# One program for attention and FFN, block 0's first layer in the drain, and DVE's turn ahead of its move

## The chip, the core and the metric

The kernel runs on one core of one Trainium2 chip. Its engines are PE (matmul), ACT (activation functions, copies), DVE (elementwise and reductions), POOL (a second elementwise engine) and SP (which only issues DMAs here). Each follows its own instruction stream in order, and semaphores tie the streams together. The metric is the device time of one execution in microseconds.

## What is computed

32 x 256 = 8192 tokens of width 128 go through attention over a memory of 4096 slots, a layer norm, a feed-forward network of width 512 and a second layer norm.

```python
q = x @ Wq.T + bq
scores = einsum('bshd,hmd->bshm', q, memory_keys) / sqrt(128)      # 8192 x 4096
probs = softmax(scores, axis=-1)
x = layernorm(x + (probs @ memory_values) @ Wo.T + bo)
h = silu((x @ w1.T) * s1) * ((x @ w2.T) * s2)                      # 128 -> 512
h = gelu((h @ h1.T) * s_h1)                                        # 512 -> 512
h = gelu((h @ h2.T) * s_h2)                                        # 512 -> 512
x = layernorm(x + (h @ w3.T) * s3)                                 # 512 -> 128
```

## The kernel before

**Two programs.** `program` calls `attention` and then `ffn`. Each opens its own block of engine programs, so all engines finish the first before any starts the second.

**Attention** works on 32 pairs of row tiles (2 x 128 tokens). `frames` runs one frame for each pair and three more to drain: frame f computes the scores of pair f while the parts of pairs f-1 and f-2 pass through the later stages. A frame has 16 steps t and, for DVE and SP, 8 slots j = 4 x tile + k, one for each piece of 1024 score columns. Frames 0 to 3 and from 28 on are written out; those between are a loop of two frames.

- *PE* (`frame`, L693): in each step three matmuls of scores (L711 to L713, high and low halves of queries and keys), and after two steps the value products of two steps of pair f-2 (`add_values`, L685 to L690). At t = 8 it projects the next pair's queries (L664).
- *DVE* (`frame`, L597): in slot j it moves the scores of piece j from PSUM to `rows` with their maximum (L608; I call it the move, M), once the previous pair's content of these rows has been sent. After the fourth move of a tile it finds the row maximum and the bias (L614, L616). Then comes the turn (T, a transpose in 32 x 32 squares, L577) of a piece that Exp has finished, by `turned_piece(f, j)`: slot 0 turns (tile 0, k 3) of the previous pair, slots 1 to 4 its tile 1, slots 5 to 7 pieces (0,0) to (0,2) of this pair.
- *SP* (`exchange`, L404): it waits for each turned piece and sends it in four DMAs of 128 KB within the SBUF from `rows` to `slot_p`, which has two halves, one for each parity of the pair. Before the first piece of a pair it waits until POOL has used up the half (L412). It also loads the queries' input and stores the outputs of pair f-3.
- *ACT* (`frame`, L508): in each step it converts a part of `slot_p` to 16 bits (`high_part`, L506; part 0 waits for all eight pieces), at even steps an Exp of a piece (L497), at t = 8 the next queries (L476).
- *POOL* (L454): the low half of each part, what the conversion lost. PE's value products need both.

The order within a step on ACT is high part, then Exp, so Exp (0,0) at t = 8 stands ahead of high part 11 of the pair before.

**Drain.** In frames 32 to 34 the last Exps, turns and exchanges of pair 31 are done, ACT issues the last exchange itself (L550), POOL makes the low halves of pair 30, DVE all of pair 31 (`last_low_part`, L582). DVE, POOL and PE already prepare the first layer norm of blocks 0 and 1.

**FFN** works on 16 blocks of 512 tokens. `turn(i)` runs, for PE, the first layer (w1, w2) of block i+1, the output transposes of block i+2, the layer h2 of block i, h1 of block i+1 and w3 of block i. Turn -1 fills the pipeline: first layer and h1 of block 0. A value read from memory (`low_max`) tells whether the weights need a low half; with these inputs they don't. DVE and PE each branch on it at the head of `ffn`.

## Time and profile before

| | |
|---|---|
| median of 3 runs | 1143.17 us (1141.53 to 1144.19) |
| the profiled execution | 1143.68 us |
| its span, first to last instruction | 1141.9 us |
| PE busy | 1092.9 us, 96% |
| DVE busy | 963.5 us, 84% |
| ACT busy | 905.3 us, 79% |
| POOL busy | 645.3 us, 57% |
| mean granted clock of PE | 0.995 |

The runs take 1.8 us more than the span from the first to the last instruction. Busy shares are means over two parts with different loads: attention to about 772 us, the FFN from 774 us on. Matmul ends are modelled by the profile, so a PE that is counted busy is not at its peak; the starts are measured.

### The profile page before, as it was taken

What the parts mean: (1) busy time and instruction counts of PE and PEld (TensorE: products, weight loads), DVE (VectorE), ACT (ScalarE), POOL (GpSimd) and SP (SyncE); (2) the same over time, 40 slices, a digit from 0 to 9 for tenths busy, and PEclk for the clock granted to TensorE, in tenths of its full rate; (3) what the DMA queues carried; (4) which work ended last, traced back from release to release, by engine and by line L of the source; (5) the groups of instructions that cost most, each with busy time, mean ns of one, the idle gap of its engine ahead of it and who ended that gap; (6) DMA issues with size and microseconds to landing.
All of it is one profiled execution on the core that took longest, in us unless ns stands there. A gap on an engine that the chain in (4) does not pass through costs nothing. (4 is left out here: it accounts for less than half of the span.)

```text
span 1141.9 us, 20141 instructions
## 1 busy us (share of the span) xinstructions
PE 1092.9 (96%) x5324; PEld 769.4 (67%) x5324; DVE 963.5 (84%) x1803; ACT 905.3 (79%) x1610; POOL 645.3 (57%) x618
## 2 busy tenths in 40 slices
PE   7799999999999999999999999988999999999996
PEld 5566666666666666666666666635787887888775
DVE  6888898998899889998998899875787887888874
ACT  6788788878887887788878877777788878888883
POOL 1487788878877887888778878760211121121110
PEclk9999999999999999999999999999999999999999
DMA  6878888888888888888888988854020111001000
GB/s 199 190 186 200 200 201 205 206 197 204 201 195 195 202 200 199 200 206 202 200 194 208 207 186 198 186 124 166 1 56 28 28 48 34 28 28 55 11 10 29
DMA packets 83942, 165.90 MB, mean 145 GB/s; under 512 B 19648, under 2 KB 47808, under 8 KB 83776
## 3 DMA queue, kind: packets, MB, share of 16 engines
q1 hardware_dynamic: 79824, 161.50, 59.8%
q10 hardware_dynamic: 4080, 3.94, 1.2%
q8 instruction: 18, 0.29, 0.1%
q14 instruction: 20, 0.16, 0.0%
HBM read 22.76 MB, written 8.39 MB: 27 GB/s over the span
## 5 line engine op out<-in xcount | busy, mean ns | idle before, releaser
L454 POOL TENSOR_TENSOR pT<-slot_p,pT 128x512 f16<-128x512 f32 x496 | 561.9, 1168 | 143.5 <-ACT pT L506 143.5
L608 DVE TENSOR_SCALAR_CACHE_REDUCE rows<-s_ps 128x1024 f32<-128x1024 f32 x256 | 310.8, 1214 | 72.9 <-DMA slot_p<-rows 48.3
L506 ACT ACTIVATE pT<-slot_p 128x512 f16<-128x512 f32 x512 | 296.1, 617 | 84.1 <-DMA slot_p<-rows 76.2
L577 DVE STREAM_TRANSPOSE rows<-rows 128x1024 f32<-128x1024 f32 x256 | 317.0, 1239 | 2.1 <-ACT rows L497 2.1
L497 ACT ACTIVATE rows<-rows,bias 128x1024 f32<-128x1024 f32 x256 | 291.6, 1139 | 15.7 <-DVE bias L616 15.4
L711 PE MATMUL s_ps<-keys,q_buf 128*128 128x512 f32 x512 | 249.6, 488 | 7.7 <-DVE rows L608 4.8
L685 PE MATMUL o_ps<-pT,v_hi 128*128 128x512 f16 x512 | 198.1, 387 | 21.2 <-POOL pT L454 20.9
L990 PE MATMUL ring<-h_hi,w_all 128*128 128x512 f32 x512 | 205.6, 402 | 1.7 <-DVE h_lo L936 1.4
L712 PE MATMUL s_ps<-keys,q_buf 128*128 128x512 f32 x512 | 203.4, 397 | 0.0
L991 PE MATMUL ring<-h_lo,w_all 128*128 128x512 f32 x512 | 202.3, 395 | 0.0
L713 PE MATMUL s_ps<-keys,q_buf 128*128 128x512 f32 x512 | 202.1, 395 | 0.0
L688 PE MATMUL o_ps<-pT,v_lo 128*128 128x256 f16 x1024 | 196.1, 273 | 0.0
L690 PE MATMUL o_ps<-pT,v_hi 128*128 128x512 f16 x512 | 194.6, 380 | 0.0
L162 POOL TENSOR_TENSOR var_eps<-moments,eps 128x4 f32<-128x4 f32 x32 | 6.8, 213 | 305.0 <-DVE moments L183 305.0
L688 PEld LDWEIGHTS o_ps<-pT,v_lo 128*128 128x128 f16 x1024 | 101.0, 99 | 83.4 <-issue 0.8
L881 ACT ACTIVATE gelu<-ring,scales 128x512 f32<-128x512 f32 x128 | 88.0, 687 | 61.8 <-PE ring L991 61.8
L685 PEld LDWEIGHTS o_ps<-pT,v_hi 128*128 128x128 f16 x512 | 49.4, 97 | 117.1 <-POOL pT L454 66.1
L711 PEld LDWEIGHTS s_ps<-keys,q_buf 128*128 128x128 f32 x512 | 96.7, 189 | 27.4 <-issue 5.1
L990 PEld LDWEIGHTS ring<-h_hi,w_all 128*128 128x128 f32 x512 | 96.2, 188 | 25.4 <-DVE h_lo L936 2.6
L713 PEld LDWEIGHTS s_ps<-keys,q_buf 128*128 128x128 f32 x512 | 96.1, 188 | 23.3
L991 PEld LDWEIGHTS ring<-h_lo,w_all 128*128 128x128 f32 x512 | 96.3, 188 | 21.6
L712 PEld LDWEIGHTS s_ps<-keys,q_buf 128*128 128x128 f32 x512 | 96.7, 189 | 17.5
(95 smaller groups left out, 1202.1 us busy)
## 6 DMA issues: line engine op xcount, KB each, us to landing
slot_p<-rows SPq DMA_DIRECT2D x1020, 128.0 KB, 2.4
x_in<-in_xT SPq DMA_DIRECT2D x32, 128.0 KB, 2.5
x_in<-in_x SPq DMA_DIRECT2D x16, 256.0 KB, 3.6
o_scratch<-o_sum SPq DMA_DIRECT2D x32, 128.0 KB, 2.0
out<-y_out SPq DMA_DIRECT2D x16, 256.0 KB, 2.4
o_in<-o_scratch SPq DMA_DIRECT2D x14, 256.0 KB, 3.3
z<-in_w_all ACTq DMA_DIRECT2D x25, 113.0 KB, 3.1
rows<-in_w_all SPq DMA_DIRECT2D x1, 2816.0 KB, 12.5
```

Of the source, the lines that this page charges most:

```text
L454: nc.gpsimd.tensor_tensor(halves(s % RING, 1), slots_first(pp, s), halves(s % RING, 0), ALU.subtract).then_inc(split, 1)
L497: nc.scalar.activation(s, s, ACT.Exp, bias=bias[:, tile:tile + 1], scale=SCALE, accum_out=den[:, bass.ds((2 * p + tile) * PIECES + k, 1)]) ...
L506: nc.scalar.activation(halves(s % RING, 0), slots_first(pp, s), ACT.Copy).then_inc(highed, 1)
L577: nc.vector.transpose(row_piece(tile, k), row_piece(tile, k)).then_inc(turned, 1)
L608: nc.vector.tensor_scalar(row_piece(tile, k), s_ps[:, j % 2, :], 1.0, None, ALU.mult, ALU.max, accum_out=part_max[:, tile, k:k + 1]).then_ ...
L685: nc.tensor.matmul(o_ps[:, pp, :], v_hi[:, 2 * s, :], pT[:, s % RING, 0, :], start=s == 0, stop=False, skip_group_check=True)
L688: nc.tensor.matmul(o_ps[:, pp, 0:2 * P], v_lo[:, 2 * s + c, :], pT[:, s % RING, c, 0:2 * P], start=False, stop=False, skip_group_check=True)
L711: nc.tensor.matmul(out, q_h, k_h, start=True, stop=False)
L712: nc.tensor.matmul(out, q_h, k_l, start=False, stop=False)
L713: last = nc.tensor.matmul(out, q_l, k_h, start=False, stop=True)
L990: nc.tensor.matmul(out, wh, hh, start=n == 0, stop=False)
L991: last = nc.tensor.matmul(out, wh, hl, start=False, stop=final and not low_weights)
```

## The change

There are three parts.

1. `attention` and `ffn` become one function `layers` with one block, so no engine waits for all others between them. The branch on `low_max` moves: PE's now stands behind frame 31, DVE has none, POOL has one. The load of the raw weights waits for the last exchanges.
2. The first layer of block 0 moves into the drain. PE does its first half behind value step 11 of pair 30 (`FIRST_LAYER_STEP`), the other half behind step 15, and h1 behind the values of pair 31. Frames 32 to 34 are written out by engine: DVE makes the low parts of pair 30 from step 12 on (`LATE_STEP`), ACT issues the last two exchanges, and ACT's gates and DVE's products of block 0 stand between high and low parts. They use free columns of `rows`. In later blocks `prod` is written over `gate`.
3. In each slot of a frame DVE turns its piece ahead of its move of scores.

Shown without the changed indentation, and cut; turns of the FFN are the same but for names and for block 0, which they no longer start:

```diff
+LATE_STEP = 12
+FIRST_LAYER_STEP = 11
...
-            for f in range(PAIRS - 4, PAIRS + 3):
+        for f in range(PAIRS - 4, PAIRS):
                 frame(f, f % 2)
...
+    def product(b, j):
+        return rows[:, (2 + j % 2) * BT:(3 + j % 2) * BT] if is_step(b, 0) else gate[:, j, :]
...
 # SP, behind its frames
+        exchange(PAIRS - 1, 1, 0, PIECES - 1)
+        exchange(PAIRS - 1, 1, 1, 0)
+        exchange(PAIRS - 1, 1, 1, 1)
+        stage.store_output(sp, PAIRS - 3)
...
+        for tile in range(2):
+            for k in range(PIECES):
+                sp.wait_ge(sent[tile][k], 16 * GROUPS * PAIRS)
+        sp.dma_start(raw, w_raw[:, 0:W_COLS]).then_inc(raw_loaded, 16)
...
 # POOL, behind its frames
+        for s in range(STEPS - T_LAG, LATE_STEP):
+            low_part(PAIRS - 2, 0, s)
             stage.inverse_deviation(pool, 1, 0)
+        pool.wait_ge(stage.low_found, 1)
+        low = pool.value_load(stage.low_max[0:1, 0:1].bitcast(I32))
+        with pool.If(low > 0):
...
+        with pool.Else():
+            nc.gpsimd.memset(table_room[:, 1:2], 0.0).then_inc(w_split, 2)
...
 # ACT, behind its frames
+        for s in range(STEPS - T_LAG, 6):
+            high_part(PAIRS - 2, 0, s)
+            if s == 3:
+                stage.output_half(act, PAIRS - 3, 1)
+        for k in range(PIECES):
+            exp_piece(PAIRS - 1, 1, k)
+        for s in range(6, STEPS):
+            high_part(PAIRS - 2, 0, s)
+            if s == 7:
+                act.wait_ge(sent[0][0], 16 * GROUPS * PAIRS)
+                stage.keep_x1T(act, 0)
+            for k in (2, 3):
+                if s == (11, 14)[k - 2]:
+                    act.wait_ge(turned, 8 * (PAIRS - 1) + PIECES + k + 1)
+                    send(act, 1, 1, k)
+        load_table(ACT.Silu)
+        act.wait_ge(stage.scales_loaded, 16 * len(scale_cols))
+        for k in (1, 2):
+            act.wait_ge(sent[0][k], 16 * GROUPS * PAIRS)
+        for j in range(2):
+            gate_of(0, j)
+        for j in range(2):
+            product_high(0, j)
+        stage.output_half(act, PAIRS - 2, 0)
+        for s in range(STEPS):
+            high_part(PAIRS - 1, 1, s)
+            if s == 8:
+                gate_of(0, 2)
+            if s == 11:
+                gate_of(0, 3)
+            if s == 13:
+                load_table(ACT.Gelu)
+                product_high(0, 2)
+        product_high(0, 3)
+        stage.output_half(act, PAIRS - 1, 1)
+        stage.keep_x1T(act, 1)
+        gelus(0, 1, mid1_done, (mid2_done, 0))
+        turns(act, turn)
...
 # DVE, in each slot of a frame
+                if valid(before[0], PAIRS):
+                    turn_piece(*before)
                     if valid(f, PAIRS):
 
                         dve.wait_ge(scored, 8 * f + j + 1)
...
-                    if valid(before[0], PAIRS):
-                        turn_piece(*before)
...
 # DVE, behind its frames
+        turn_piece(PAIRS - 1, 0, PIECES - 1)
+        turn_piece(PAIRS - 1, 1, 0)
+        stage.output_sum(dve, PAIRS - 3, 1)
+        for k in range(1, PIECES):
+            turn_piece(PAIRS - 1, 1, k)
                         stage.split_x1(dve, 0)
+        for s in range(LATE_STEP, STEPS):
+            low_part(PAIRS - 2, 0, s)
+        stage.residual(dve, 1)
+        dve.wait_ge(stage.scales_loaded, 16 * len(scale_cols))
+        for j in range(2):
+            product_of(0, j)
+        for j in range(2):
+            product_low(0, j)
                         for s in range(STEPS):
-                            last_low_part(s, 1 - par)
+            low_part(PAIRS - 1, 1, s)
+            if s == 5:
                         stage.normalise_x1(dve, 1)
+            if s == 8:
+                product_of(0, 2)
+            if s == 11:
+                product_of(0, 3)
+            if s == 13:
+                product_low(0, 2)
+        product_low(0, 3)
+        stage.output_sum(dve, PAIRS - 2, 0)
+        stage.output_sum(dve, PAIRS - 1, 1)
+        stage.sum_rows(dve, READY_TILES, TILES, 1)
+        dve.wait_ge(stage.rden_ready, 2)
+        gelu_low(0, 1, 0)
+        gelu_low(0, 1, 1)
+        stage.split_x1(dve, 1)
+        gelu_low(0, 1, 2)
+        gelu_low(0, 1, 3)
+        turns(dve, turn)
...
 # PE, behind its frames
+        def last_values(low_weights):
+
+            for s in range(STEPS):
+                add_values(PAIRS - 2, 0, s)
+                if s == (STEPS - 1 if low_weights else FIRST_LAYER_STEP):
+                    pe.wait_ge(scores_moved, 8 * PAIRS)
+                    pe.wait_ge(stage.w_rounded, CHECKS)
+                    pe.wait_ge(stage.x1_split, 1)
+                    if low_weights:
+                        pe.wait_ge(w_split, 1)
+                    first_layer(0, (0, 1), low_weights)
+            first_layer(0, (2, 3), low_weights)
+            for s in range(STEPS):
+                add_values(PAIRS - 1, 1, s)
+            stage.turn_x1(pe, 1)
+            if low_weights:
+                pe.wait_ge(w_split, 2)
+            for j in range(HC):
+                bank_read_by_in(0, j)
+                layer(ring[:, j, :], "h1", j, 0, mid1_done, low_weights, parts_ready=(in_split, 0))
+
+        pe.wait_ge(stage.low_found, 1)
+        low = pe.value_load(stage.low_max[0:1, 0:1].bitcast(I32))
+        with pe.If(low < 1):
+            last_values(False)
+            turns(pe, lambda i, i2, par: turn(i, i2, par, False))
```

## Rows read from the trace of the kernel before

**Rows 1.** The windows of a stretch of attention and of one FFN turn.

```profile
500.00:650.00 150.00, 148.28 (x756) 98.36 (x753) 135.84 (x207) 123.87 (x233) 122.66 (x112) 1.00 0.87 202
...
833.50:855.50 22.00, 22.00 (x102) 17.64 (x101) 17.99 (x50) 18.07 (x29) 3.71 (x5) 1.00 0.13 36
```

**Rows 2.** The waits of 100 to 600: total us, times, longest.

```profile
DVE rows L608 <- DMA slot_p<-rows: 36.6, 41, 1.9
...
PE o_ps L685 <- POOL pT L454: 8.7, 18, 0.8
ACT rows L497 <- DVE bias L616: 8.3, 14, 0.9
```

**Rows 3.** SP's own waits, 100 to 600, then 640 to 760.

```profile
SPq L376 <- POOL pT L454: 13.0, 20, 1.0
SPq L376 <- DVE rows L577: 7.7, 24, 0.6
...
SPq L376 <- DVE rows L577: 7.1, 8, 2.0
```

**Rows 4.** The timeline of one frame, 400 to 427, four engines.

```profile
403.83 1.22 DVE L608 TENSOR_SCALAR_CACHE_REDUCE rows<-s_ps 128x1024 f32<-128x1024 f32 x1 [1.79 <-DMA slot_p<-rows]
...
407.95 1.15 ACT L497 ACTIVATE rows<-rows,bias 128x1024 f32<-128x1024 f32 x1 [0.86 <-DVE bias L616]
...
409.79 5.65 POOL L454 TENSOR_TENSOR pT<-slot_p,pT 128x512 f16<-128x512 f32 x5 [2.21 <-ACT pT L506]
...
415.46 3.05 SPq L376 DMA_DIRECT2D slot_p<-rows  x5
...
426.97 1.22 DVE L608 TENSOR_SCALAR_CACHE_REDUCE rows<-s_ps 128x1024 f32<-128x1024 f32 x1 [1.86 <-DMA slot_p<-rows]
```

**Rows 5.** DVE's timeline: first and last of 21 such moves.

```profile
174.78 1.23 DVE L608 TENSOR_SCALAR_CACHE_REDUCE rows<-s_ps 128x1024 f32<-128x1024 f32 x1 [0.87 <-DMA slot_p<-rows]
...
630.90 1.23 DVE L608 TENSOR_SCALAR_CACHE_REDUCE rows<-s_ps 128x1024 f32<-128x1024 f32 x1 [0.83 <-DMA slot_p<-rows]
```

**Rows 6.** PE's timeline: the first matmul of two neighbouring slots.

```profile
406.14 0.58 PE L711 MATMUL s_ps<-keys,q_buf 128*128 128x512 f32 x1
...
408.85 0.59 PE L711 MATMUL s_ps<-keys,q_buf 128*128 128x512 f32 x1
```

**Rows 7.** The timeline around a frame's end, ACT and DVE.

```profile
416.52 0.63 ACT L506 ACTIVATE pT<-slot_p 128x512 f16<-128x512 f32 x1 [2.18 <-DMA slot_p<-rows]
417.06 1.14 ACT L497 ACTIVATE rows<-rows,bias 128x1024 f32<-128x1024 f32 x1
...
419.65 1.23 DVE L608 TENSOR_SCALAR_CACHE_REDUCE rows<-s_ps 128x1024 f32<-128x1024 f32 x1 [0.43 <-DMA slot_p<-rows]
```

**Rows 8.** The timeline of the drain, engine by engine.

```profile
748.88 11.81 POOL L454 TENSOR_TENSOR pT<-slot_p,pT 128x512 f16<-128x512 f32 x10 [1.88 <-ACT pT L506]
...
749.86 1.08 DVE L198 SCALAR_TENSOR_TENSOR z<-y_ps,rden,xb 128x128 f32<-128x128 f32 x4
...
759.96 10.30 DVE L582 TENSOR_TENSOR pT<-slot_p,pT 128x512 f16<-128x512 f32 x16 [5.83 <-ACT pT L506]
770.18 1.10 DVE L188 TENSOR_SCALAR x<-z,moments,rstd 128x128 f32<-128x128 f32 x4
...
775.75 0.75 DVE L930 SCALAR_TENSOR_TENSOR prod<-ring,scales,gate 128x512 f32<-128x512 f32 x1 [0.89 <-ACT gate L865]
...
753.47 2.19 ACT L506 ACTIVATE pT<-slot_p 128x512 f16<-128x512 f32 x4 [1.59 <-PE o_ps L690]
...
768.11 1.28 ACT L553 ACT_TABLE_LOAD   x1
...
774.05 0.49 PE L990 MATMUL ring<-keys,w_all 128*128 128x512 f32 x1 [2.09 <-DVE spare L914]
...
775.45 0.63 PE L991 MATMUL ring<-keys,w_all 128*128 128x512 f32 x1
...
789.41 0.40 PE L990 MATMUL ring<-keys,w_all 128*128 128x512 f32 x1
```

More of the change, by code:

```diff
@@ new lines, in layers @@
+    wo_power, wo_scale, wo_scaled = (stage.xb[:, n, :] for n in range(3))
+    ident, v_unscale, o_ps = stage.ident, stage.v_unscale, stage.o_ps
+    spare_half = slot_p[:, 1, :, :, :].rearrange("p a c t -> p (a c t)")
+    k_raw = spare_half[:, 0:SLOTS]
+    v_in = spare_half[:, SLOTS:2 * SLOTS]
+    v_raw = k_raw
+    s_ps = ctx.enter_context(nc.psum_tensor("s_ps", [P, 2, PIECE], FP32))
+    q_ps = stage.x1_ps
+    k_loaded = [sem(f"k_loaded{n}") for n in range(K_PARTS)]
+    v_loaded = [sem(f"v_loaded{n}") for n in range(PIECES)]
@@ new lines, in part_step, with value_halves, checking, check_part @@
+    def part_step(f, t, lag):
+        return (f - 1, t - lag) if t >= lag else (f - 2, t + STEPS - lag)
+    def value_halves(f, t):
+        step = t - V_STEP + STEPS * f if isinstance(f, int) else -1
+        return (step,) if 0 <= step < HALVES else ()
+    def checking(f):
+        return not isinstance(f, int) or 0 <= f - FIRST_CHECK < CHECKS
+    def check_part(f):
+        return stage.w_all[:, bass.ds((f - FIRST_CHECK) * CHECK_COLS, CHECK_COLS)]
+    def slots_first(pp, s):
+        return slot_p[:, pp, :, 2 * s:2 * s + 2, :].rearrange("p a c t -> p c a t")
@@ new lines, in halves, with k_part, frames, send @@
+    def halves(t, low):
+        return pT[:, t, :, low * 2 * P:(low + 1) * 2 * P].rearrange("p c (a t) -> p c a t", t=G)
+    def k_part(t, n):
+        return half_piece(t, n) if n < 2 else piece(t, n - 1)
+    def frames(eng, frame):
+        for f in range(4):
+            frame(f, f % 2)
+        with eng.Fori(2, PAIRS // 2 - 2) as half:
+            frame(half * 2, 0)
+            frame(half * 2 + 1, 1)
+        for f in range(PAIRS - 4, PAIRS):
+            frame(f, f % 2)
+    def send(eng, pp, tile, k):
+        for g in range(GROUPS):
+            eng.dma_start(slot_p[k * G:(k + 1) * G, pp, tile * GROUPS + g, :, :].rearrange("p c t -> p (c t)"),
+                          row_piece(tile, k)[g * G:(g + 1) * G, :]).then_inc(sent[tile][k], 16)
@@ new lines, in layers @@
+    ctx.close()
+    ctx = hold
+    w_hi = stage.w_all[:, 0:W_COLS]
+    in_room = keys[:, 2 * BT:2 * BT + 2 * HC * BT].rearrange("p (a k n) -> p a k n", a=2, k=HC)
+    w_lo_in = keys[:, 2 * BT + 2 * HC * BT:2 * BT + 2 * HC * BT + W_AT["h1"]]
+    w_lo_rest = sb("w_lo_rest", [P, W_COLS - W_AT["h1"]], FP32R)
+    raw = rows[:, 2 * SLOTS - W_COLS:]
+    x1T, x1_hi, x1_lo, scales, table_room = stage.x1T, stage.x1_hi, stage.x1_lo, stage.scales, stage.table_room
+    gelu = sb("gelu", [P, 2, HC, BT], FP32)
@@ L1050, in turn @@
-                if valid(i, BLOCKS):
-                    at_least(pe, z2T_ready, i)
-                    layer(y3_ps[:, :], "w3", 0, 2, y3_done, low_weights, P, (gelu_split[1], 4 * i))
-            with pe.If(stage.low_of["PE"] < 1):
-                turns(pe, lambda i, i2, par: turn(i, i2, par, False))
-            with pe.Else():
-                turns(pe, lambda i, i2, par: turn(i, i2, par, True))
+                        bank_read_by_in(i + 1, j)
+                    else:
+                        pe.wait_ge(gelu_h[0], 4 * i + j + 1)
@@ L1072, in program @@
         stage = RowStage(nc, stage_ctx, t["x"].rearrange(tiled, p=P), o_dram, o_stored, den, keys, rows)
[L1073 to L1075 removed]
+        layers(nc, stage, stage_ctx, t["xT"], t["wqT"], t["bq"], t["kT"], t["vT"], t["woT"], t["bo"], scale_cols, t["w_all"],
+               den, keys, rows, out.rearrange(tiled, p=P))
 def kernel(**inputs):
```

1246 lines of the change are left out of this document (580 added, 666 removed).

## The prediction

> **What bounds the kernel now.** I read the windows first. In the attention part every engine but PE has idle time, and PE is counted busy nearly throughout; in the FFN part PE is busy in 22.00 of 22.00 us and nothing else is near that [rows 1]. So an FFN turn costs 22.0 us as long as PE is fed, and the diff changes nothing inside a turn: sixteen turns stay as they are. What can move is the period of a pair of row tiles in attention, and the drain between the last scores and the first FFN turn.
>
> The period comes from the starts of one instruction in successive frames: DVE's move of the third piece of scores, which I call M2. Its starts run from 174.78 to 630.90 with 20 periods between, so 22.81 us a pair [rows 5]. PE could do it in less: one slot (scores of a piece, then two value steps) starts 2.71 us after the one before [rows 6], eight make 21.7 us, the projection of the next queries adds about 0.4 (my estimate from one slot that holds it), so PE's floor is about 22.1 to 22.2 us. The period is 0.6 to 0.7 above it.
>
> Next the waits, for what holds the period up. Over 500 us (22 pairs) PE waits 8.7 us for the low half of the probabilities, 0.40 a pair; DVE waits 36.6 us for the landing of exchanges, 1.7 a pair; ACT waits for the bias before an Exp in 14 pairs [rows 2]. SP, which issues 32 exchanges of 128 KB a pair, idles only 0.35 us a pair for a turn of DVE and 0.6 for POOL [rows 3]. Nearly everything is close to full, so single idle times prove little and a closed loop has to be found.
>
> The timeline gives one [rows 4]. M2 starts at 403.83, when the previous pair's piece (0,2) has left its rows. A turn, the next move M3, the maximum and the bias follow, and ACT's Exp of piece (0,0) starts at 407.95. Behind this Exp in ACT's order stands high part 11, behind that POOL's last five subtracts: they start at 409.79 and take 5.65, to 415.44. They free the half of slot_p, and SP, which waited for exactly that, issues (0,0) at 415.46. Then come (0,1), an input and (0,2), and its landing starts M2 of the next frame at 426.97. That is 4.12 + 1.84 + 5.65 + 11.53 = 23.14 us, all of this pair's period and no other engine in it. Where the bias is waited for (14 of 22 pairs) this loop is the bound; in the rest PE's query projection arrives a little later than the bias and decides.
>
> **The change, part by part.**
>
> *DVE's turn ahead of its move.* The cyclic order of M and T (turn) is the same, each T steps over one M, so each T can be done one move earlier, up to 1.2 us. Gain on the last exchange (1,3): SP loses its 0.35 us a pair of waiting for DVE, high part 0 starts that much sooner, and the 0.40 us a pair that PE waits at the second value step mostly goes. But in the loop above nothing gets shorter: M2 waits for the DMA in every frame, and between M2 and M3 there still stands one T, now (1,2) in place of (1,1). What PE gains it will wait for M2 or M3 in the scores. I cost the edit at zero in the pairs that the loop binds and at about 0.15 us (estimate) in the 8 of 22 that PE's projection binds, so -1 us over the main part. Its lower bound is the PE floor (rival B), its upper bound a T that waits for its Exp and holds up the M behind it (rival D).
>
> In the unrolled frames 28 to 31 DVE carries extra work (block 0's residual and statistics), and SP waits for turns 7.1 us between 640 and 760, up to 2.0 at a time, part of it in the drain [rows 3]. Turns that are one move early give back between 0 and 4 of this; the loop above still stands behind it, so I take 1.5, nearer to the low end.
>
> *The drain, before.* POOL's ten subtracts for steps 6 to 15 of pair 30 run from 748.88 for 11.81 us; DVE then does all 16 of pair 31 from 759.96 for 10.30; then a normalisation, 1.10. PE has its last value step done at 774.05 - 2.09 = 771.96, waits 2.09 through the end of the first program and the branch of the second, and only then begins block 0's first layer; turn 0 proper, block 1's first layer, begins at 789.41 [rows 8]. At 775.45 a matmul takes 0.63: the granted clock of that stretch is at the lower of the two levels (1.2 GHz) after the pause, and that costs about 1.5 us before 779. So 17.4 us pass between the last value step and turn 0.
>
> *The drain, after.* POOL ends its share with step 11, at 748.88 + 6 x 1.18 = 756.0. PE puts the first half of block 0's first layer behind step 11 (8 matmuls, 1.9 us by the rate of a turn), then steps 12 to 15 (0.65 each, as two fill about half of a slot of 2.71 [rows 6]), to about 761.2. ACT now issues two pieces between its high parts; today's one cost it 1.59 us ahead of high part 12, seen at 753.47 [rows 8]. The second should cost 1.6 to 3 more, since its sequencer runs ahead I take high part 15 done at 757.1. Then the table load 1.28 (row at 768.11) and two gates, done at 759.3 and 760. DVE does lows 12 to 15 to 757.7, then the residual, whose combinations take 1.08 [rows 8] and the statistics about as much again (estimate 2.4 in all, 760.1), two products of 0.75, to 761.7. ACT's copies and its output half follow, two subtracts of up to 0.75 run beside them, and high part 0 of pair 31 is ready at about 763.4. This is 3.5 us later than today's 759.96.
>
> From there DVE sets the pace: 10.30 + 1.10 + three operations of 0.75 (products 2 and 3, one low part) = 13.65 us, to 777.1; PE's last value step follows at 777.7. So the values end 5.8 us later than before. What is behind them is shorter: no pause of 2.09, no first layer of block 0, only block 1's transposes (0.5) and 32 matmuls of the second layer. A turn has 102 instructions, 88 of them of this size, in 22.00 us [rows 1], so one is 0.22 to 0.25 and 32 take 6.9 to 8.0; I take 7.6. The 16 of the first layer that are gone from here were 3.5 to 4.0, and 1.5 more by the clock. Turn 0 begins at 785.9 instead of 789.41: -3.5 us. With each estimate above at its better or worse end this is -6.5 to 0.
>
> The cover of what I cost at nothing: PE's value load and branch now stand ahead of pair 30's values. All of today's pause, 2.09, bounds them, and PE would be at most 0.7 late for step 0; the steps come at POOL's 1.18 each and PE needs 0.65, so it has caught up by the third. The Trainium skill (Runtime: NRT & Kernel Launch, Instruction fetch mechanics) says that a taken branch whose target is not in the fetched window stalls the engine for a fetch. That speaks for a price at the new place too; by it the sum stays the same, because of the cover. The trace shows only the pause of 2.09, barrier and branch together. POOL's branch and its memset have nothing waiting in this path; the raw weights' load, now behind the landing of all exchanges, is needed only in turn 1.
>
> *Sum.* -1.0 - 1.5 - 3.5 = -6.0. The span of 1141.9 becomes 1135.9, the profiled execution's 1143.68 becomes 1137.7. The median of the runs is 0.5 below that execution, so **1137**.
>
> **The rivals.** Differences under 0.2% (2.3 us) can hardly be told from no change.
>
> A, as above: 1132 to 1140.9. For it: M2 waits for the DMA in all the frames I followed. Chance 0.54.
>
> B, the attention period falls. If the loop has slack that I misread (landing after (0,2) shorter when (1,3) has left the queues sooner), the period can fall from 22.81 towards PE's 22.2: 0.6 x 27 = 16 us at most, to 1121; half of it gives 1129. For it: PE's wait and SP's for DVE are both removed, and every engine has idle time. Against it: the stretch from SP's (0,0) to M2 holds the same three pieces. Chance 0.18.
>
> C, the drain gives nothing. DVE's 13.65 us are a chain with ACT's gates; if gates wait for the late issue of two pieces, or the granted clock falls to the lower level in the DVE-paced values as at 775.45, the 3.5 us go, and with them part of the rest: 1140 to 1144. Chance 0.17.
>
> D, slower. One mechanism: T(0,3) now stands ahead of M0. Its Exp starts only after high part 0, which waits for the exchange: 416.52, Exp 417.06 to 418.19, T to 419.4, and M0 starts at 419.65 [rows 7]. The margin is 0.2 us. If the Exp slips by x, M0 and M1 slip by x - 0.2, but M2 has 1.7 us of waiting in hand, so this decides only from x of about 1.5 on. At 2 us a pair it costs 0.3 x 27 = 8 us: 1145 to 1149. Chance 0.11.
>
> Faster: A 0.54, B 0.18, a part of C 0.03, together 0.75. Same: the rest of C, mostly, 0.13. Slower: D and a little of C, 0.12. The range takes in A, nearly all of C and the nearer half of B: 1125 to 1143; A alone is 1132 to 1141.
>
> **What would show it.** M2's starts stay 22.6 to 22.8 us apart, with the DMA as what it waited for, while PE's wait for POOL at the second value step shrinks below 0.15 a pair and SP's wait for DVE nearly vanishes. DVE's 16 last subtracts start at 763 to 764 less the shift of about 2.5 that comes from ahead, and PE's first matmul of block 1 comes about 6 us earlier than 789.41. A period of 22.3 would prove the loop wrong; a DVE wait for L497's Exp ahead of a turn in most frames would be rival D; a lower granted clock between 760 and 785 or a PE pause over 1 us behind the last value step would be C.

## The result, and the profile after

The changed kernel takes 1125.84 us, median of 4 runs (1123.78 to 1126.36); the kernel before took 1142.9 beside it (1141.53 to 1144.19). The ratio is 0.9848, 95% interval 0.983 to 0.9865: 17.1 us less, where 6.0 were predicted. The range of 1125 to 1143 holds the time by 0.8 us, but the likeliest case, A (1132 to 1140.9), does not. The profiled execution has a span of 1122.1 us against 1141.9, so 19.8 us less.

The windows of the changed kernel, in the columns of [rows 1]: the same stretch of attention, and one turn of the FFN.

```profile
core 0: us, PE busy (x) PEld busy (x) DVE busy (x) ACT busy (x) POOL busy (x), PEclk, DMA share, GB/s
500.00:650.00 150.00, 147.95 (x761) 99.65 (x761) 135.63 (x205) 124.64 (x233) 125.72 (x115) 1.00 0.89 205
819.81:841.56 21.75, 21.75 (x101) 17.64 (x100) 17.96 (x50) 18.07 (x30) 3.71 (x5) 1.00 0.13 36
```

PE is busy throughout in both, as before. The turn, however, is 21.75 long and not 22.00. Its waits from 100 to 600, to be read against [rows 2]:

```profile
DVE rows L812 <- DMA slot_p<-rows: 27.3, 45, 1.5
...
PE o_ps L972 <- POOL pT L542: 7.5, 12, 0.8
...
ACT rows L613 <- DVE bias L820: 3.6, 11, 1.0
```

SP's own waits in that stretch, against [rows 3]:

```profile
SPq L377 <- POOL pT L542: 13.9, 16, 1.3
SPq L377 <- DVE rows L779: 9.8, 30, 0.6
```

I had said that SP's wait for DVE would nearly vanish and PE's for POOL shrink from 0.40 a pair to 0.15. Neither happened: 9.8 in place of 7.7 us, and 7.5 in place of 8.7. What became less is DVE's wait for the DMA (36.6 to 27.3) and ACT's for the bias (8.3 to 3.6).

The starts of M2, the move that the prediction took the period from, against [rows 5] (the same 20 periods):

```profile
172.53 1.22 DVE L812 TENSOR_SCALAR_CACHE_REDUCE rows<-s_ps 128x1024 f32<-128x1024 f32 x1 [1.52 <-DMA slot_p<-rows]
...
622.79 1.22 DVE L812 TENSOR_SCALAR_CACHE_REDUCE rows<-s_ps 128x1024 f32<-128x1024 f32 x1 [1.05 <-DMA slot_p<-rows]
```

That is 22.51 us a pair, in place of 22.81. I had expected 22.6 to 22.8, and 22.3 as the proof that the loop is wrong; it lies between the two.

For a ledger I cut each trace at three marks: ACT's conversion of the queries of pair 4 and of pair 31 (`q_buf`), and the transposes into `y_ps` in turn 0. The marks of before, ACT's timeline:

```profile
63.55 0.47 ACT L476 ACTIVATE q_buf<-x_ps,bq_col 128x256 fp32r<-128x256 f32 x1 [1.52 <-PE x_ps L664]
85.85 0.47 ACT L476 ACTIVATE q_buf<-x_ps,bq_col 128x256 fp32r<-128x256 f32 x1 [1.18 <-PE x_ps L664]
...
705.84 0.47 ACT L476 ACTIVATE q_buf<-x_ps,bq_col 128x256 fp32r<-128x256 f32 x1 [1.22 <-PE x_ps L664]
```

And of the changed kernel, with three neighbouring pairs of the loop:

```profile
61.79 0.47 ACT L592 ACTIVATE q_buf<-x_ps,bq_col 128x256 fp32r<-128x256 f32 x1 [0.95 <-PE x_ps L951]
83.87 0.48 ACT L592 ACTIVATE q_buf<-x_ps,bq_col 128x256 fp32r<-128x256 f32 x1 [1.76 <-PE x_ps L951]
...
581.40 0.47 ACT L592 ACTIVATE q_buf<-x_ps,bq_col 128x256 fp32r<-128x256 f32 x1 [1.29 <-PE x_ps L951]
603.57 0.47 ACT L592 ACTIVATE q_buf<-x_ps,bq_col 128x256 fp32r<-128x256 f32 x1 [1.70 <-PE x_ps L951]
626.30 0.47 ACT L592 ACTIVATE q_buf<-x_ps,bq_col 128x256 fp32r<-128x256 f32 x1 [1.29 <-PE x_ps L951]
...
695.84 0.48 ACT L592 ACTIVATE q_buf<-x_ps,bq_col 128x256 fp32r<-128x256 f32 x1 [1.22 <-PE x_ps L951]
```

The `y_ps` transposes of turn 0 start at 791.50 before and at 776.31 after. So the 19.8 us are: 2.0 ahead of pair 4, 8.0 in the 27 periods to pair 31 (620.0 to 612.0), 5.2 from there to turn 0 (85.7 to 80.5), and 4.6 in the FFN (350.4 to 345.8). From about pair 10 to the end of the loop every other period is now 22.17 us, which is the PE floor of 22.1 to 22.2 that the prediction worked out, and the ones between are 22.7 to 23.0.

### The profile page after: what moved, and what is told of

Its sections match the earlier page's. It is cut to its first block, busy times and chain, and to the rows that moved or that the text cites. A ratio compares the mean times of both kernels' runs of the same rounds, so it can differ in the third digit from the quotient of the medians.

```text
span 1122.1 us, 20046 instructions
## 1 busy us (share of the span) xinstructions
PE 1081.3 (96%) x5324; PEld 770.6 (69%) x5324; DVE 968.3 (86%) x1806; ACT 905.3 (81%) x1609; POOL 642.1 (57%) x615
## 4 chain that ended last, share of the span: by engine, by line
PE 36%; SPq 15%; ACT 13%; issue 10%; DVE 9%; POOL 8%; DMA 7%; ACTq 1%; DVEq 0%; POOLq 0%
SPq L377 14%; PE ring L1045 12%; PE ring L1046 12%; POOL pT L542 7%; ACT rows L613 7%; DMA slot_p<-rows 6%; ACT pT L622 5%; DVE rows L812 3%; DVE rows L779 3%; PE o_ps L1045 1%; PE o_ps L1046 1%; PE s_ps L1000 1%; PE s_ps L998 1%; PE s_ps L999 1%; PE o_ps L972 1%
## 5 line engine op out<-in xcount | busy, mean ns | idle before, releaser
L542 POOL TENSOR_TENSOR pT<-slot_p,pT 128x512 f16<-128x512 f32 x482 | 545.7, 1166 | 130.5 <-ACT pT L622 130.5
L812 DVE TENSOR_SCALAR_CACHE_REDUCE rows<-s_ps 128x1024 f32<-128x1024 f32 x256 | 308.6, 1205 | 51.8 <-DMA slot_p<-rows 34.7
L613 ACT ACTIVATE rows<-rows,bias 128x1024 f32<-128x1024 f32 x256 | 291.7, 1140 | 12.6 <-DVE bias L820 12.0
L975 PEld LDWEIGHTS o_ps<-pT,v_lo 128*128 128x128 f16 x1024 | 101.1, 99 | 84.2 <-issue 0.6
L1045 PE MATMUL ring<-keys,w_all 128*128 128x512 f32 x384 | 153.3, 399 | 1.0 <-ACT gate L669 0.9
L1046 PE MATMUL ring<-keys,w_all 128*128 128x512 f32 x384 | 150.5, 392 | 0.0
L1000 PEld LDWEIGHTS s_ps<-keys,q_buf 128*128 128x128 f32 x512 | 96.3, 188 | 22.7
L876 DVE TENSOR_TENSOR h_lo<-gelu,h_hi 128x512 fp32r<-128x512 f32 x128 | 81.9, 688 | 26.5 <-ACT h_hi L698 26.3
L1045 PE MATMUL ring<-h_hi,w_all 128*128 128x512 f32 x256 | 103.1, 403 | 0.3 <-ACT gate L669 0.3
```

The costliest lines, as they stand in the source:

```text
L542: nc.gpsimd.tensor_tensor(halves(s % RING, 1), slots_first(pp, s), halves(s % RING, 0), ALU.subtract).then_inc(split, 1)
L613: nc.scalar.activation(s, s, ACT.Exp, bias=bias[:, tile:tile + 1], scale=SCALE, accum_out=den[:, bass.ds((2 * p + tile) * PIECES + k, 1)]) ...
L812: nc.vector.tensor_scalar(row_piece(tile, k), s_ps[:, j % 2, :], 1.0, None, ALU.mult, ALU.max, accum_out=part_max[:, tile, k:k + 1]).then_ ...
L975: nc.tensor.matmul(o_ps[:, pp, 0:2 * P], v_lo[:, 2 * s + c, :], pT[:, s % RING, c, 0:2 * P], start=False, stop=False, skip_group_check=True)
L1000: last = nc.tensor.matmul(out, q_l, k_h, start=False, stop=True)
L1045: nc.tensor.matmul(out, wh, hh, start=n == 0, stop=False)
```

## The experiments

The runs came in groups, each on one chip, and the kernel before reads 1138.2 to 1143.1 us in median from group to group. So times are compared by their ratio to the before of the same group, and stretches by the traces. This is the ledger of all profiled runs, in us (cut as above; "order" is DVE's, new is turn ahead of move):

| run | order, programs | to pair 4 | pair 4 to 31 | to turn 0 | FFN | ratio (95%) |
|---|---|---|---|---|---|---|
| before | old, 2 | 85.85 | 620.0 | 85.7 | 350.4 | 1 |
| g1_before_again | old, 2 | 86.19 | 616.6 | 87.4 | 350.7 | 0.9998 (0.998 to 1.0015) |
| e6_pad_alone | old, 2 | 86.02 | 618.8 | 87.3 | 350.2 | 0.9983 (0.9966 to 1.0001) |
| f1_ffn_edits_alone | old, 2 | 87.45 | 613.9 | 85.6 | 345.7 | 0.9957 (0.994 to 0.9973) |
| e1_reorder_alone | new, 2 | 84.47 | 614.4 | 84.2 | 350.4 | 0.9954 (0.9939 to 0.9969) |
| e2_order_undone | old, 1 | 85.74 | 613.1 | 82.2 | 345.7 | 0.9895 (0.9878 to 0.9911) |
| f2_order_undone_no_pad | old, 1 | 87.85 | 615.5 | 81.0 | 346.3 | 0.9922 (0.9905 to 0.994) |
| f3_order_at_start_only | both, 1 | 84.13 | 614.0 | 81.5 | 345.8 | 0.9901 (0.9885 to 0.9918) |
| changed kernel | new, 1 | 83.87 | 612.0 | 80.5 | 345.8 | 0.9848 (0.983 to 0.9865) |
| e5_changed_again | new, 1 | 84.05 | 612.4 | 80.8 | 345.8 | 0.9859 (0.9831 to 0.9887) |
| h2_changed_control | new, 1 | 84.73 | 613.1 | 81.0 | 346.0 | 0.9851 (0.9837 to 0.9865) |
| e3_two_waits_more | new, 1 | 83.99 | 612.5 | 80.2 | 347.3 | 0.9878 (0.9861 to 0.9894) |
| e4_own_room | new, 1 | 84.45 | 611.9 | 81.1 | 347.9 | 0.9886 (0.9869 to 0.9902) |
| e7_no_pad | new, 1 | 84.04 | 614.0 | 80.0 | 345.9 | 0.9862 (0.9834 to 0.989) |
| e8_small_work_later | new, 1 | 84.33 | 613.3 | 79.9 | 345.7 | 0.9859 (0.9831 to 0.9887) |
| f4_h2_high_in_keys | new, 1 | 84.45 | 613.5 | 80.4 | 344.8 | 0.9867 (0.9851 to 0.9884) |
| g2_pool_all_lows | new, 1 | 84.16 | 613.0 | 79.8 | 345.9 | 0.9869 (0.9851 to 0.9888) |
| g3_sp_sends_one_more | new, 1 | 84.10 | 611.4 | 80.3 | 345.7 | 0.9855 (0.9834 to 0.9875) |
| g4_first_layer_behind | new, 1 | 85.38 | 613.9 | 87.0 | 345.6 | 0.9917 (0.9895 to 0.9939) |
| h1_both | new, 1 | 84.28 | 613.1 | 79.9 | 345.7 | 0.9845 (0.9831 to 0.986) |

**The order of DVE, alone and taken back.** e1 is the kernel before with the turn ahead of the move; e2 is the changed kernel with this undone:

```diff
                 if j == PIECES and valid(f + 1, PAIRS):
                     q_low_part(f + 1, 1 - par)
+                if valid(before[0], PAIRS):
+                    turn_piece(*before)
                 if valid(f, PAIRS):
                     ...
-                if valid(before[0], PAIRS):
-                    turn_piece(*before)
```

> The kernel before with DVE's reorder alone (turn ahead of move in each slot), two programs, drain and FFN as before. Theory P (the one-frame loop of the prediction: M2, bias, Exp (0,0), high part 11, POOL, SP (0,0), landing, M2): 1 to 2.5 us less than before, about 1141. Theory Q (a chain over two frames: M3, bias, query low part, then T(1,3), its exchange, high part 0, sixteen low parts of POOL, SP (0,0), M2; before, M4 stood in it ahead of T(1,3)): the whole attention gain of the change, 2 at the start and 0.27 a pair, so about 10 us less, 1133, and frames of 22.2 and 22.9 us in turn. If the gain needs one program, nothing here.

> The changed kernel with DVE's move of scores ahead of the turn again, all else of the change kept. Theory Q: the 10 us of attention come back, about 1136, period 22.8. Theory P: 1 to 2.5 come back, about 1128. What is left against before is the worth of the drain and the FFN: 5.2 + 4.6 by the two traces, so 9.8 less than before (1133) if these add up independently of the order, and 3.5 if the drain is worth what was predicted and the FFN nothing.

e1 took 1134.78 against 1139.83, 5.05 less, and e2 1128.33, 11.5 less. Their sum, 16.6, is about what the whole change saves (17.1 in its own group, 16.5 in that of e5), so the order on one side and drain with FFN on the other add up. Neither theory had the size of e1: P said 1 to 2.5, Q about 10. The stretch ahead of pair 4 is settled by these and by the next run.

**Where the order acts.** f3 keeps the new order in frames 0 to 3 and has the old one behind.

```diff
-                if valid(before[0], PAIRS):
+                if valid(before[0], PAIRS) and isinstance(f, int) and f < 4:
                     turn_piece(*before)
...
+                if valid(before[0], PAIRS) and not (isinstance(f, int) and f < 4):
+                    turn_piece(*before)
```

> The changed kernel with the new order of DVE in frames 0 to 3 only, the old one in the loop and behind. Theory O: of the 3.0 us between the changed kernel and the old order, 1.7 arise in frames 2 to 4 (frame 3's queries at 61.8 instead of 63.5), 0.7 in the loop and the rest in the drain: about 1126.6 if the start's gain is kept. Rival P (the loop absorbs what the start gains, since all stages wait for each other): 1128.3, as with the old order everywhere.

It took 1127.18. All six kernels with the old order at the start have pair 3's queries 24.2 to 25.7 us after pair 2's, and all with the new one, f3 too, 22.4 to 22.5: a gain of 1.7 or more that is still there at pair 4 (f3 reaches it at 84.13). Whether it lasts to the end the times don't tell: f3's ratio, 0.9901, lies between those of e2 and f2, which have the old order everywhere. The rows of POOL's first low part show how. Before:

```profile
51.23 1.16 POOL L454 TENSOR_TENSOR pT<-slot_p,pT 128x512 f16<-128x512 f32 x1 [13.18 <-ACT pT L506]
```

After:

```profile
48.87 1.16 POOL L542 TENSOR_TENSOR pT<-slot_p,pT 128x512 f16<-128x512 f32 x1 [10.73 <-ACT pT L622]
```

POOL's first low part is 2.4 us earlier; it starts at 51.2 to 51.8 in all traces with the old order and at 48.9 to 50.3 in all with the new. My explanation, which no run takes apart, is that while the pipeline fills no loop of freed buffers stands behind the turns, so that an earlier turn brings the exchange, the high part and what follows forward.

**Is it a chain through T(1,3)?** e8 moves two small operations of DVE (0.39 and 0.47) from the stretch between bias and T(1,3) to slot 6.

```diff
-                if j == PIECES and valid(f + 1, PAIRS):
-                    q_low_part(f + 1, 1 - par)
...
-                if j == 3 and checking(f - 1):
+                if j == 6 and checking(f - 1):
...
+                if j == 6 and valid(f + 1, PAIRS):
+                    q_low_part(f + 1, 1 - par)
```

> The changed kernel with DVE's two small operations between bias and T(1,3) (maximum of the weight check, 0.39; query low part, 0.47) moved to slot 6 behind the move. Theory Q (two-frame chain through T(1,3)): the longer of the two frames, 22.9, comes down towards 22.17, by up to 0.37 a pair, so 4 to 10 us less than the changed kernel. Rival R (SP, which issues for about 21.4 of 22.5 us, or PE's floor is the bound): nothing, within 1 us.

> The changed kernel again, on the chip of the next three runs, as their reference. 0.9848 of before, so 1123 to 1126; turns of the FFN 21.73 apart, frames 22.17 and 22.9 in turn.

e8 took 1125.16, e5 1125.23. Theory Q, which I had formed after the result, fell: its chain got 0.86 us shorter and nothing moved.

**Addresses and chance.** `table_room` moves all buffers behind it by 32 bytes. e6 adds such a buffer to the kernel before, e7 and f2 take it out of the changed kernel and of e2.

```diff
         self.spare = sb("spare", [P, 2], FP32)
+        self.pad = sb("pad", [P, 2], FP32)
```

> The kernel before with nothing but an unused buffer of two float32 columns, declared where the change declares table_room. All later buffers of SBUF, those of attention among them (values, slot_p, pT, the queries), lie 32 bytes further, on multiples of 64 bytes, which they do not before. Theory A (the 32 bytes shorten attention: the changed kernel with the old order of DVE had 22.54 us a pair against 22.81 before, with the same instructions in the loop): about 7 us less than before, first layer etc. unchanged, matmul slots of 2.69 in place of 2.71. Rival: that gain comes from the one program or is chance, and this kernel runs as before.

> The changed kernel with table_room inside the buffer spare, so that nothing of attention is moved by 32 bytes. Theory A: the PE-bound frames take 22.28 in place of 22.17, as in the run with the reorder alone, and 3 us are lost against the changed kernel, which leaves about 1128. Rival: as the changed kernel.

> The changed kernel with DVE's old order and with table_room inside spare, so that attention has the old addresses and, instruction for instruction, the old streams as far as frame 31. Theory O (in one program the new order is worth 3 us, addresses 0.5 at most): 1128 to 1129, all runs within 1 us, attention 613 us from the queries of frame 4 to those of the last. Rival N (attention of the old order varies by chance from kernel to kernel, 613 to 620): anything to 1135, with a spread as wide as that of before (8 us).

> The kernel before, unchanged. Theory V (the attention of the old order varies from execution to execution, and the trace of before was near its slow end): between the queries of frame 4 and the last 613 to 617 us, not 620, and a time under 1141. Rival: 619 to 621 again, so that the gain against the kernels with the old order in one program is due to something that the one program changes.

e6: 1140.22 against 1141.7, no difference. e7: 1125.65, as e5. Only the PE-bound periods feel it, 22.28 (e1, e7) and 22.17 (with the 32 bytes), 0.11 in every other pair, about 1.5 us. f2 took 1130.39 with runs from 1127.93 to 1132.38, so the one program with the old order isn't always as steady as in e2 (1127.61 to 1128.55). g1, the kernel before unchanged, took 1141.89 and has 616.6 from pair 4 to 31. With the old order that stretch is thus 613 to 620 long whatever else changes, and [rows 5] come from its longest sample; with the new order it is 611.4 to 614.4. The two ranges overlap, so a single pair of traces says little about the order here.

**The FFN's turn.** e3 gives DVE back the two waits ahead of each product, e4 puts the parts of h1's input into buffers of their own, f1 makes the edits of the FFN alone in the kernel before.

```diff
 # e3
             dve.wait_ge(in_done, 8 * b + 2 * j + 2)
+            if not is_step(b, 0):
+                dve.wait_ge(prod_high, 4 * b + j - 3)
+                dve.wait_ge(in_split, 4 * b + j - 3)
 # e4
+    own_hi, own_lo = sb("h_hi0", [P, HC, BT], FP32R), sb("h_lo0", [P, HC, BT], FP32R)
 # f1
-        prod = sb("prod", [P, HC, BT], FP32)
-        h_hi = sb("h_hi", [P, 3, HC, BT], FP32R)
+        prod = gate
+        in_room = keys[:, SLOTS:2 * SLOTS].rearrange("p (a k n) -> p a k n", a=2, k=HC)
+        h_hi = [in_room[:, 0, :, :]] + [sb(f"h_hi{n}", [P, HC, BT], FP32R) for n in (1, 2)]
...
-                        at_least(dve, prod_high, 4 * b + j - 3)
-                        at_least(dve, in_split, 4 * b + j - 3)
```

f1 takes the keys' second half for that room, where the low parts of the weights would lie that these inputs don't need.

> The changed kernel with the two waits given back to DVE ahead of each product of blocks 1 to 15 (both always satisfied). Theory W (each wait instruction costs DVE about 0.07 us, and PE waits for the second product of a turn): 0.15 us a turn in 15 turns, 2.3 us more, about 1128, turn 21.9. Rival S (the shorter turn comes from where the operands lie): no change, 1126.

> The changed kernel with the high and low parts of the first layer's product in buffers of their own from block 1 on, in place of the room of the keys. Theory S (matmuls of layer h1 start 0.2275 apart when their operand lies in the keys' room and 0.2335 elsewhere): 0.12 to 0.19 us a turn, 2 to 3 us more, about 1128. Rival W: no change, 1126.

> The kernel before with two edits of the FFN alone: the product is written over the gate, so that DVE has two waits less ahead of each, and the parts of layer h1's input lie in the keys' room. Theory F (both together are the whole shortening of a turn, 0.14 + 0.15 us as the two runs that took one of them back showed): turns of 21.73 us, 16 x 0.3 = 4.6 us less than before, drain and attention as before, about 1137. Rival: a turn is shorter only in the one program, no change.

f1 took 1133.67 against 1138.22, 4.55 less, as expected. The ratios of e3 and e4 (0.9878 and 0.9886) are hardly apart from the changed kernel's, so for them the traces decide. The turns of the traces show both parts. Between the transposes into `y_ps` and those of `z2T` stands the second half of the first layer. DVE's rows there, before:

```profile
837.29 1.41 DVE L930 SCALAR_TENSOR_TENSOR prod<-ring,scales,gate 128x512 f32<-128x512 f32 x2 [1.00 <-ACT gate L865]
```

In the changed kernel:

```profile
821.64 1.41 DVE L856 SCALAR_TENSOR_TENSOR gate<-ring,scales,gate 128x512 f32<-128x512 f32 x2 [0.84 <-ACT gate L669]
```

And in e3:

```profile
822.22 1.41 DVE L859 SCALAR_TENSOR_TENSOR gate<-ring,scales,gate 128x512 f32<-128x512 f32 x2 [1.00 <-ACT gate L669]
```

The operation is the same; its idle time ahead is 0.16 longer with four waits than with two, and PE, which waits for this product, takes 2.46, 2.30 and 2.46 us for the stretch. PE's rows show where the time goes although the engine counts as busy. Before:

```profile
837.81 0.39 PE L991 MATMUL ring<-keys,w_all 128*128 128x512 f32 x1
838.10 0.50 PE L990 MATMUL ring<-keys,w_all 128*128 128x512 f32 x1
838.43 0.39 PE L991 MATMUL ring<-keys,w_all 128*128 128x512 f32 x1
```

After:

```profile
822.33 0.39 PE L1046 MATMUL ring<-keys,w_all 128*128 128x512 f32 x1
822.55 0.40 PE L1045 MATMUL ring<-keys,w_all 128*128 128x512 f32 x1
822.78 0.39 PE L1046 MATMUL ring<-keys,w_all 128*128 128x512 f32 x1
```

The three starts span 0.62 us before and 0.45 after. The longer stretch is found in the ten turns of the loop; in the written-out turns it is 2.29 in all three kernels. What differs there is that the waits are against constants and not against a running count, so it is probably the running count that costs. e3's FFN is 1.5 us longer.

From the `x_ps` transposes to w3 stand 24 matmuls of h1: 6.04 us before and in e4, 5.91 in the changed kernel, e3 and f1. PE's rows before:

```profile
853.60 0.39 PE L990 MATMUL ring<-h_hi,w_all 128*128 128x512 f32 x1
853.84 0.40 PE L991 MATMUL ring<-h_lo,w_all 128*128 128x512 f32 x1
854.07 0.39 PE L990 MATMUL ring<-h_hi,w_all 128*128 128x512 f32 x1
```

After:

```profile
838.34 0.39 PE L1045 MATMUL ring<-keys,w_all 128*128 128x512 f32 x1
838.56 0.39 PE L1046 MATMUL ring<-keys,w_all 128*128 128x512 f32 x1
838.79 0.39 PE L1045 MATMUL ring<-keys,w_all 128*128 128x512 f32 x1
```

In the last twelve of the 24, the mean over the turns is 0.2267 from start to start with the operand in the room of the keys and 0.2333 elsewhere, both at the full granted clock. In the first half the room of the keys gives 0.227 to 0.235, so the short spacing isn't a property of the place alone. e4's FFN is 2.2 us longer.

Together e3 and e4 give 3.7 of the 4.6 back. The rest is one wait in a written-out turn, which stands in the traces of before, g1, e6 and e1 and in none with both edits or with one of them:

```profile
1070.36 0.66 PE L226 MATMUL x_ps<-ident,x 128*128 128x128 f32 x4 [0.65 <-DVE x L188]
```

From its `z2T` transposes to this row pass 10.59 us, against 9.75 in the changed kernel, 0.8 more. What removes it wasn't isolated: e3 and e4 both keep the product written over the gate. f4 puts the high parts of h2's input there too:

```diff
-    h_hi = [in_room[:, 0, :, :]] + [sb(f"h_hi{n}", [P, HC, BT], FP32R) for n in (1, 2)]
+    room_1 = keys[:, 8 * BT + 4 * BT:8 * BT + 8 * BT].rearrange("p (k n) -> p k n", k=HC)
+    h_hi = [in_room[:, 0, :, :], room_1, sb("h_hi2", [P, HC, BT], FP32R)]
```

> The changed kernel with the high parts of layer h2's input in the last 2048 columns of the keys as well. Theory S (a matmul whose moving operand lies there is followed 0.2267 later instead of 0.2334): 16 of the 32 matmuls of h2, 0.11 us a turn, 1.6 less than the changed kernel, about 1123.7. Rival: the short spacing belongs to layer h1 or needs both parts there, no change.

It took 1123.51, its ratio is not apart from the changed kernel's, and h2's stretch is 9.63 in some turns and 9.83 to 9.91 in others, against 9.82. So half the operands there give a part of it in some turns and nothing in others; why the place matters stays open.

**The drain.** The rows of the changed kernel, against [rows 8]: POOL, DVE, ACT and PE.

```profile
737.83 8.70 POOL L561 TENSOR_TENSOR pT<-slot_p,pT 128x512 f16<-128x512 f32 x6 [1.87 <-ACT pT L622]
...
741.72 3.80 DVE L784 TENSOR_TENSOR pT<-slot_p,pT 128x512 f16<-128x512 f32 x3 [0.90 <-ACT pT L622]
...
753.08 3.68 DVE L784 TENSOR_TENSOR pT<-slot_p,pT 128x512 f16<-128x512 f32 x6
...
742.25 3.04 ACTq L377 DMA_DIRECT2D slot_p<-rows  x3
745.34 0.63 ACT L622 ACTIVATE pT<-slot_p 128x512 f16<-128x512 f32 x1 [2.61 <-issue]
...
766.27 0.38 PE L977 MATMUL o_ps<-pT,v_hi 128*128 128x512 f16 x1
...
766.85 0.48 PE L1045 MATMUL ring<-keys,w_all 128*128 128x512 f32 x1
...
774.22 0.39 PE L1045 MATMUL ring<-keys,w_all 128*128 128x512 f32 x1
```

POOL's six subtracts take 1.45 each and DVE's three 1.27 while they run side by side; DVE alone takes 0.61 (3.68 for six). The Trainium skill (SBUF — State Buffer, Who interferes with whom) says that a DVE operation on two tensors with both inputs in SBUF contends with GpSimd's reads; these rows agree. ACT's issue of two pieces holds its own high part 15 up for 2.61.

Three runs ask what matters of this: g2 lets POOL make all low parts of pair 30, g3 lets SP send one of ACT's pieces, g4 puts block 0's first layer, gates and products behind the values of pair 31; h1 joins g2 and g3.

```diff
 # g2
-LATE_STEP = 12
+LATE_STEP = 16
 # g3
         exchange(PAIRS - 1, 1, 1, 1)
+        exchange(PAIRS - 1, 1, 1, 2)
...
-            for k in (2, 3):
-                if s == (11, 14)[k - 2]:
+            for k in (3,):
+                if s == 14:
 # g4, PE; ACT's gates and DVE's products likewise
-                if s == (STEPS - 1 if low_weights else FIRST_LAYER_STEP):
-                    ...
-                    first_layer(0, (0, 1), low_weights)
-            first_layer(0, (2, 3), low_weights)
             for s in range(STEPS):
                 add_values(PAIRS - 1, 1, s)
+            first_layer(0, (0, 1), low_weights)
+            first_layer(0, (2, 3), low_weights)
```

> The changed kernel with LATE_STEP = 16: POOL makes the low parts of pair 30 to the end, DVE only those of pair 31. Theory C (side by side both are slower: POOL's six took 1.45 each, DVE's four 1.27 to 1.08 instead of 0.64, so sharing gains little): POOL at 1.17 each is done with step 15 at about 749.6, the first half of the first layer comes 1.5 us earlier, and turn 0 moves by less than 1 us either way; 1124.5 to 1126. Rival: DVE's help is worth what it takes off POOL, 4 x 1.17 us less what DVE spends, and without it the kernel is 2 to 3 us slower.

> The changed kernel with SP sending piece (1,2) of pair 31 and ACT only (1,3). ACT's 2.61 us of waiting for its own queue ahead of high part 15 go. Theory L (that late high part holds low part 15, and through it the residual, the products and the low parts of pair 31): DVE's subtracts of pair 31 begin 1 to 1.5 us earlier and the kernel gains as much, 1124. Rival (POOL's step 11 and the gates set the pace, and SP's later landing takes it back): within 0.5 us of the changed kernel.

> The changed kernel with the first layer of block 0, its gates and products behind the values of pair 31 again, but in the one program, without barrier or pause. By the rows of before: from the first layer to turn 0 15.36 us less 1.5 of the lower clock, 13.9, and the values end about 5 us earlier than in the changed kernel, at 761.2; turn 0 at about 775.1 instead of 774.2. Theory B (most of the drain's gain is the barrier's pause and the clock): 1 us slower than the changed kernel, 1126. Theory I (most of it is the weaving): 3 to 5 us slower.

> The changed kernel with SP sending piece (1,2) of pair 31 and with LATE_STEP = 16. In the traces of each alone, turn 0 came 0.2 to 0.5 and 0.7 to 1.0 us sooner behind the last queries. If they add up, 0.9 to 1.5 us less than the changed kernel on the same chip. Rival: once SP's landing or DVE's low parts of pair 31 set the pace they don't add, and it is within 0.5 us.

> The changed kernel once more, as the reference of the run beside it: 0.985 to 0.987 of before, 612 to 613 us from the queries of frame 4 to the last, frames of 22.17 and 22.9 us in turn.

g2 took 1125.96, g3 1123.96, against 1125 to 1126 of the changed kernel in other groups; the stretch to turn 0 is 1.0 and 0.4 shorter than its mean of 80.8 over the changed kernel's three traces. g3's ratio, 0.9855, is that of the changed kernel, and its DVE starts the subtracts of pair 31 only 0.4 to 0.8 sooner behind the last queries than the changed kernel does, so theory L isn't borne out; g2 agrees with its theory C. Together, and on one chip, h1 took 1124.93 against 1126.20 of h2: 1.3 us less, with ranges that overlap (to 1125.92, from 1125.31) and the stretch 1.1 shorter.

g4 was the surprise: 1132.34, ratio 0.9917, some 7 us more than the changed kernel. Its stretch to turn 0 is 87.0, no shorter than in the kernels with two programs (85.6 to 87.4 with the old order, 84.2 with the new one that g4 has). Its windows:

```profile
750.00:760.00 10.00, 7.31 (x35) 3.81 (x34) 8.06 (x25) 6.29 (x14) 2.50 (x4) 0.83 0.99 336
760.00:770.00 10.00, 10.00 (x60) 6.53 (x59) 6.53 (x11) 4.64 (x8) 0.00 (x0) 1.00 0.17 71
770.00:780.00 10.00, 7.45 (x27) 5.14 (x26) 6.48 (x13) 7.49 (x13) 0.00 (x0) 0.83 0.04 13
```

And PE's rows behind a wait for the first layer's low parts:

```profile
776.08 0.50 PE L1039 MATMUL ring<-keys,w_all 128*128 128x512 f32 x1 [2.34 <-DVE keys L860]
776.42 0.59 PE L1040 MATMUL ring<-keys,w_all 128*128 128x512 f32 x1
...
777.27 0.63 PE L1040 MATMUL ring<-keys,w_all 128*128 128x512 f32 x1
```

Without the barrier there still is a pause, 2.34 of waiting for the low parts of DVE's products, and behind it the granted clock falls to the lower level, as at 775.45 in [rows 8]. It falls in the window from 750 too, where PE waited 2.69 for DVE's first low part of pair 31:

```profile
755.96 0.61 PE L966 MATMUL o_ps<-pT,v_hi 128*128 128x512 f16 x1 [2.69 <-DVE pT L781]
```

The changed kernel in three windows:

```profile
740.00:750.00 10.00, 7.97 (x35) 3.83 (x35) 8.55 (x20) 5.99 (x10) 6.93 (x7) 0.86 0.92 254
750.00:760.00 10.00, 9.33 (x54) 5.56 (x53) 9.96 (x18) 9.36 (x18) 2.60 (x3) 1.00 0.88 332
770.00:780.00 10.00, 9.02 (x40) 6.56 (x38) 5.90 (x9) 8.07 (x14) 0.00 (x0) 1.00 0.21 61
```

The granted clock is 1.00 in the last two: PE does the first layer while DVE makes low parts, and gates and products are done when PE needs them. Among the values of pair 30 (740 to 750) the clock is below 1.00 here as well, as it is in g4.

g4 isn't the kernel before without its barrier, though. Its first matmul of the first layer stands right behind the last value step (767.85 behind 767.82), so the 2.09 of the barrier are gone, but its values end 2.8 us later behind the last queries than before (last matmul at 68.5 against 65.7), and the stretch from the start of the first layer to turn 0 is 1 us longer (16.3 against 15.36).

## Why the prediction was wrong in size

**Main attention, -1.0, and frames 28 to 31, -1.5: the order's own effect was about right, but two things were missed.** From pair 4 to 31 the order is worth 1.8 us in one program (614.3, the mean of two traces, and 612.5 of the changed kernel's three; 1.4 with f3 and all twelve traces of the new order) and 2.9 in two (617.3 and 614.4, the latter one trace); 2.5 were predicted. Behind pair 31 it gives 0.9 to 2.3 more. Rivals: of B's 16 us at most the pair of traces has half (8.0), but by the means over the traces it is 4.8 and by the order alone 1.8 to 2.9, though every other period reached PE's floor; D fell, DVE waits for L613 ahead of a turn for at most 0.4 us. That my loop is the reason was not tested as such, and three of its signs (SP's wait, PE's wait, the period of M2) were wrong; that the size is near may be luck. First miss: the fill. I looked at periods from 174 us on; the order also gives 2.2 ahead of pair 4 (means 86.5 and 84.3 over the runs). Second: in the traces of one program that stretch is shorter even with the old order (613.1 and 615.5, against 613.9 to 620.0), though the instructions and waits as far as frame 31 are the same. It is 2 to 3 us. Part of it is chance, since the trace of before was the longest of four; whether a part is the one program stays open.

**"A turn stays as it is", 0: wrong, -4.6.** This was the step that failed outright. The diff did change a turn, and the description ahead of the prediction ("the same but for names and for block 0") missed it: two waits fewer ahead of each product, in a stretch where PE waits for that product, and h1's operand in another place. With one edit taken back in each, e3 gave 1.5 and e4 2.2 of it back, 0.8 is the one wait at 1070.36, and f1 showed the sum alone, 4.55. I had read that PE was busy in 22.00 of 22.00 and took that as a floor; but a matmul that follows late is given a longer row (0.50 in place of 0.39 at 838.10 above), so a busy PE hid 0.17 there.

**The drain, -3.5: it gave 5.2 in the pair of traces, and 3.5 where the order is the old one (e2 against before; 4.3 against the mean of the four traces with two programs, 86.5).** By the prediction's steps: DVE's subtracts of pair 31 were to begin 3.5 later than the row of before less the 10.0 that come from ahead, 750.0, and began at 753.08, 3.1 later. They and what stands between were to take 13.65 and took 12.6 (to 765.7). The last value matmul starts at 766.27 and its row ends at 766.65; that is 4.7 later than the shifted 771.96, not 5.8. From there to turn 0 I had 8.2, measured 7.6 (to 774.22), with 32 matmuls in 7.37. So each step held within 1.1, on the better side, and the term was too small by 1.7: 1.1 up to the end of the values and 0.6 behind it. What I had wrong is why they pay. I credited the pause and the clock, as things that the barrier causes; g4, which has no barrier and keeps the layer behind the values, gained nothing over two programs (87.0 against 84.2 to 87.4). On top of the rest of the change the weaving is thus worth 6 us (87.0 against 80.8), the two stretches of lower clock in it. What the barrier's removal is worth by itself isn't shown, since g4 keeps the new split of the low parts.

**The covers.** PE's value load and branch ahead of pair 30's values cost nothing. The first matmul of pair 30 stands right behind the last of pair 29:

```profile
730.07 0.38 PE L977 MATMUL o_ps<-pT,v_hi 128*128 128x512 f16 x1
730.28 0.38 PE L972 MATMUL o_ps<-pT,v_hi 128*128 128x512 f16 x1
```

That is the 0.21 to 0.22 of any step from one matmul to the next. The rule on taken branches that the prediction weighed (the Trainium skill, Runtime: NRT & Kernel Launch, Instruction fetch mechanics) would put a gap here if this branch is taken out of the fetched window, which no trace shows; there is no gap. Rival C (the clock at its lower level in the DVE-paced values) did not come.

The sum as it was, from the means: fill 2.2, main part 4.8 (of it 1.8 to 2.9 the order), drain 5.7, FFN 4.6, together 17.3 of the 17.1 measured.

## What to carry to other kernels

Before calling a stage unchanged, count each engine's wait instructions and the place of each operand in the diff, even where the bound engine reads as fully busy. When an order is changed in a pipelined loop, cost the fill apart from the steady state, since what the loop absorbs the fill keeps. A pause on PE is best removed by giving it independent work there; a barrier that merely goes may leave a wait of the same size on the next product, as the 2.34 of g4 for the 2.09 of before.

## What the runs showed of the hardware

- Waits that are satisfied can cost time: two more ahead of a DVE operation made its idle time 0.16 us longer in the loop, where they are made against a running count (PE's stretch 2.46 against 2.30), and not in written-out turns, where the count is a constant (2.29).
- The last twelve matmuls of h1 (512 columns) started 0.2267 us apart with the moving operand in one buffer and 0.2333 with it in another (e4). A shift of all attention buffers by 32 bytes took the PE-bound period from 22.28 to 22.17.
- Thirteen executions of the kernel before ran from 1138.2 to 1146.7 in one group, and four of the changed one beside it from 1124.8 to 1125.9.
